# Splitting row maxima into bfloat16 parts by two truncating subtractions instead of four instructions, in a two-layer attention and feed-forward kernel

## The reference

```python
x = x + _L0_xattn_ref(_layernorm(x), ctx_2048, ...)   # attention in a band of 64, 8 heads of 8
x = x + _L0_ffn_ref(_layernorm(x), weight, scale)     # 256x256 product, row norm, tanh gain
x = x + _L1_xattn_ref(_layernorm(x), ctx_2048, ...)   # cross attention with rotary positions
x = x + _L1_ffn_ref(_layernorm(x), ...)               # 256 -> 1024 -> 256, relu, low-rank parts
```

## Time and profile before

| | |
|---|---|
| time, median of 3 runs | 1358.02 us (1356.0 to 1359.34) |
| the profiled execution | 1357.87 us, span of its instructions 1356.1 us |
| TensorE busy | 1272.2 us, 94% of the span |
| VectorE, ScalarE, GpSimd busy | 930.4, 854.8 and 709.6 us |
| attention of layer 0, steady part | about 100 to 500 us; an iteration takes some 15.5 us |
| attention of layer 1, steady part | about 620 to 1100 us; an iteration takes 15.5 us at first and 15.1 us later |
| last feed-forward | about 1140 us to the end |

### The profile page before, as it was taken

How to read it: one execution, slowest core, us unless ns; L and a number is a source line. 1 busy time by engine, 2 the same in 40 slices (tenths; PEclk the granted TensorE clock), 3 DMA queues, 4 the chain that set the end, 5 groups by cost and what they waited for, 6 DMA issues and landing times.

```text
span 1356.1 us, 36204 instructions
## 1 busy us (share of the span) xinstructions
PE 1272.2 (94%) x11164; PEld 833.3 (61%) x11164; DVE 930.4 (69%) x2052; ACT 854.8 (63%) x1849; POOL 709.6 (52%) x1297
## 2 busy tenths in 40 slices
PE   6999999999999997768999999999999989999998
PEld 3666666666666665544555556666666546666665
DVE  6888888888888874649899978888888852111110
ACT  2566666666667675556788878888888772222111
POOL 4577778777777865046555645556555410100000
PEclk9999999999999998987999989999999999999999
DMA  8554454444445440024344444444444400000000
GB/s 207 119 131 110 107 114 114 105 109 113 111 109 117 91 96 7 12 63 92 86 104 106 94 88 98 100 104 108 95 100 104 102 3 1 31 16 15 15 15 31
DMA packets 90487, 113.35 MB, mean 84 GB/s; under 512 B 13971, under 2 KB 80275, under 8 KB 82739
## 3 DMA queue, kind: packets, MB, share of 16 engines
q1 hardware_dynamic: 89216, 111.25, 35.2%
q10 hardware_dynamic: 1206, 1.29, 0.3%
HBM read 18.66 MB, written 4.19 MB: 17 GB/s over the span
## 4 chain that ended last, share of the span: by engine, by line
PE 75%; DVE 10%; issue 4%; POOL 4%; DMA 3%; ACT 3%; SPq 1%; POOLq 0%; DVEq 0%; ACTq 0%
PE bank L475 14%; PE bank L435 13%; PE bank L451 12%; PE bank L696 8%; PE bank L687 8%; PE bank L433 6%; PE bank L487 3%; DVE row_max L1136 3%; PE bank L506 2%; PE bank L538 2%; PE bank L527 2%; PE bank L516 2%; DMA Ks<-Ks 1%; PE bank L549 1%; PE bank L645 1%
## 5 line engine op out<-in xcount | busy, mean ns | idle before, releaser
L1136 DVE TENSOR_REDUCE row_max<-bank 128x2 f32<-128x384 f32 (+1 forms) x1024 | 594.4, 616 | 106.8 <-PE bank L435 102.9
L732 ACT ACTIVATE probs<-bank 128x384 f32<-128x384 f32 (+1 forms) x1024 | 539.5, 542 | 173.4 <-PE bank L451 160.3
L435 PE MATMUL bank<-Ks,Qs 96*128 96x192 bf16 (+1 forms) x2048 | 372.9, 264 | 11.3 <-DMA Ks<-Ks 6.2
L451 PE MATMUL bank<-Qs,Ks 128*128 128x192 bf16 (+1 forms) x2048 | 366.4, 260 | 13.7 <-ACT probs L732 12.4
L1360 POOL TENSOR_SCALAR_AFFINE_SELECT probs<-probs 128x256 f32<-128x256 f32 (+1 forms) x512 | 259.2, 530 | 112.4 <-ACT probs L732 91.9
L435 PEld LDWEIGHTS bank<-Ks,Qs 96*128 96x128 bf16 x2048 | 185.6, 99 | 126.8 <-DVE row_max L1136 43.1
L475 PE MATMUL bank<-probs,V 128*32 128x192 f32 (+1 forms) x4096 | 248.4, 360 | 5.4 <-POOL probs L1360 3.8
L451 PEld LDWEIGHTS bank<-Qs,Ks 128*128 128x128 bf16 x2048 | 185.7, 98 | 48.2 <-ACT probs L732 34.5
L433 PE MATMUL bank<-band,ident 128*128 128x384 bf16 x512 | 168.7, 330 | 2.5 <-DMA Ks<-Ks 2.0
L475 PEld LDWEIGHTS bank<-probs,V 128*32 128x32 f32 x4096 | 107.4, 109 | 84.4 <-issue 37.8
L1297 DVE TENSOR_TENSOR X<-bank,X 128x256 f32 (+1 forms) x32 | 13.6, 424 | 185.6 <-PE bank L696 185.6
(11 more groups left out here) (118 smaller groups left out, 1670.6 us busy)
## 6 DMA issues: line engine op xcount, KB each, us to landing
Ks<-Ks SPq DMA_DIRECT2D x64, 576.0 KB
Qs<-Qs SPq DMA_DIRECT2D x128, 192.0 KB
Qs<-Qp SPq DMA_DIRECT2D x192, 64.0 KB
Ks<-Kp SPq DMA_DIRECT2D x192, 64.0 KB
X<-in_x SPq DMA_DIRECT2D x4, 1024.0 KB, 13.4
side<-in_ctx_crossed SPq DMA_DIRECT2D x32, 128.0 KB, 2.1
side<-in_ctx SPq DMA_DIRECT2D x32, 128.0 KB, 2.1
out<-X SPq DMA_DIRECT2D x8, 512.0 KB, 3.0
```

What stands on the lines that cost most here:

```text
L435: last = nc.tensor.matmul(dst[:, blk * win:(blk + 1) * win], Qs[0:SHIFT_ROW, pair[1], h, blk * P:(blk + 1) * P], Ks[0:SHIFT_ROW, pair[1], ...
L451: last = nc.tensor.matmul(dst[:, blk * win:(blk + 1) * win], Ks[:, pair[1], h, blk * P:(blk + 1) * P], Qs[:, pair[1], h, start(blk):start( ...
L732: nc.scalar.activation(probs[:, h % 8, 0:2 * win], exp_bank[h % 2][:, 0:2 * win], ACT.Exp, scale=SCALE).then_inc(s["exped"], 1)
L1136: nc.vector.tensor_reduce(row_max[:, pair[1], h, :], bank_of(pair, h)[:, 0:2 * win].rearrange("p (b k) -> p b k", b=2), AX.X, ALU.max).the ...
```

## The change

The parts are now kept in float32 beside each other in `row_max`, which has a plane for each part, and the bfloat16 part is the *upper half* of each float32 number, read in place with a step of two (`upper`). The high part of a number is so its float32 form cut off at 16 bits, not rounded, and needs no instruction. The middle part is the upper half of `x - upper(x)`, and the last is the upper half of what the second subtraction leaves. Two of four instructions are left, `max_rest` and `max_last`. The wait for the turn of the pair before, which protected the old buffer, is gone, since `row_max` has room for three pairs.

```diff
-        row_max = sb("row_max", [P, RING, HPP, 2])
-        max_parts = sb("max_parts", [P, 2, PARTS, HPP], bf16)
-        max_rest = sb("max_rest", [P, 2, HPP])
+        row_max = sb("row_max", [P, RING, 2, PARTS, HPP])
...
+        def upper(part):
+
+            return part.bitcast(bf16)[:, 1::2]
...
-                for here in (slice(0, CH), slice(CH, P)):
+                for here in (slice(0, CH), slice(CH, P)) if l == 0 else (slice(0, P),):
                     last = nc.tensor.matmul(job_bank["B"][here, 0:T], w[here, WO, here], mixed_in[here, :],
                                             start=True, stop=True)
...
-                nc.tensor.transpose(max_bank[b], max_parts[:, half, :, :].rearrange("p n h -> p (n h)"),
+                nc.tensor.transpose(max_bank[b],
+                                    upper(row_max[:, pair[1], half, :, :].rearrange("p n h -> p (n h)")),
                                     ident16[:, :]).then_inc(s[f"{b}_filled"], 1)
...
-        def split_max(e, engine, s, l, pair, half):
+        def max_rest(e, engine, s, pair, half):
...
+            parts = row_max[:, pair[1], half, :, :]
+            wait_apart(e, (s["maxed"], num(pair) * HPP + HEADS * (half + 1)))
+            engine.tensor_tensor(parts[:, 1, :], parts[:, 0, :], upper(parts[:, 0, :]),
+                                 ALU.subtract).then_inc(s[f"max_step{half}"], 1)
+
+        def max_last(e, engine, s, pair, half):
...
+            parts = row_max[:, pair[1], half, :, :]
+            wait_apart(e, (s[f"max_step{half}"], num(pair) + 1))
+            engine.tensor_tensor(parts[:, 2, :], parts[:, 1, :], upper(parts[:, 1, :]),
                                  ALU.subtract).then_inc(s[f"max_parts{half}"], 1)
...
                     if l == 0 and h in (0, HEADS):
-                        split_max(e, nc.vector, s, l, p1 if h else r, 1 - h // HEADS)
+                        max_rest(e, nc.vector, s, p1 if h else r, 1 - h // HEADS)
+                    if l == 0 and h in (1, HEADS + 1):
+                        max_last(e, nc.vector, s, p1 if h > 1 else r, 1 - h // HEADS)
...
                     split("q", p3, Qp, q_rest, "q_mid", "q_parts")
-                    split_max(e, nc.gpsimd, s, l, p1, 0)
+                    max_rest(e, nc.gpsimd, s, p1, 0)
+                    max_last(e, nc.gpsimd, s, p1, 0)
                     split("k", p3, Kp, k_rest, "k_mid", "k_parts")
-                    split_max(e, nc.gpsimd, s, l, p1, 1)
+                    max_rest(e, nc.gpsimd, s, p1, 1)
+                    max_last(e, nc.gpsimd, s, p1, 1)
```

More of the change, by code:

```diff
@@ L985, in _ @@
                 relu_chunk(i * 2 + 1, 1)
-        def split_max(e, engine, s, l, pair, half):
+        def max_rest(e, engine, s, pair, half):
             if not active(pair):
                 return
[L991 to L1003, removed]
+            parts = row_max[:, pair[1], half, :, :]
[3 more added lines that the diff above has]
+        def max_last(e, engine, s, pair, half):
+            if not active(pair):
+                return
+            parts = row_max[:, pair[1], half, :, :]
+            wait_apart(e, (s[f"max_step{half}"], num(pair) + 1))
+            engine.tensor_tensor(parts[:, 2, :], parts[:, 1, :], upper(parts[:, 1, :]),
                                  ALU.subtract).then_inc(s[f"max_parts{half}"], 1)
@@ L1135, in maximum @@
                 e.wait_ge(s["scored"], num(pair) * HPP + h + 1)
-                nc.vector.tensor_reduce(row_max[:, pair[1], h, :],
+                nc.vector.tensor_reduce(row_max[:, pair[1], h // HEADS, 0, h % HEADS * 2:h % HEADS * 2 + 2],
                                         bank_of(pair, h)[:, 0:2 * win].rearrange("p (b k) -> p b k", b=2),
```

## The result

The changed kernel takes 1341.26 us (median of its runs) against 1358.43 us for the one before, measured beside it: a ratio of 0.9871, 95% interval 0.9849 to 0.9892. The profiled execution took 1342.02 us.

The account below looks back on a forecast made before the run. TensorE was taken as the bound in both attentions. Gains of 6.2 (layer 0's turn), 7.2 (projection) and 2.2 us (layer 1's split) sum to 15.6; from 1357.87 that gives 1342.3, rounded up to 1343 us, range 1337 to 1354.

Parts of the forecast that it names:

- The turn of half 1 in layer 0: TensorE's wait for the split on VectorE, shortened by 0.21 us a pair: 6.2 us over some 30 pairs.
- The turn of half 0: In layer 0, the turn at step 12 was said to have no wait to save: nothing gained.
- four steps of scores later: In layer 0, half 0's split at step 8 precedes its turn at step 12, so a shorter split saves nothing.
- VectorE's freed time: nothing: In layer 0, two copies fewer per split free VectorE, at 83.5% not the bound: no gain.
- The output projection: In layer 1, the step across it falls from 0.90 to 0.66 us: 0.24 a pair, 7.2 us for 30 pairs.
- the shorter split: On GpSimd in layer 1, parts 0.44 us earlier stay in time for step 12's turn, which TensorE reaches 0.24 earlier.
- rival 1: In layer 1 another engine, VectorE or ScalarE, takes the gain; only layer 0's 6.2 us remain: 1351.7 us, chance 0.14.
- The earlier turn in layer 1: Half 0's turn waits less for GpSimd's split: 0.24 us in 9 early pairs, 2.2 us; later iterations nothing.
- straight on: In layer 1's later iterations ScalarE goes from its copy directly to the exponentials, so an earlier turn gains nothing.
- the 9.4 us that were forecast for it: Layer 1's gain: 7.2 us from the output projection and 2.2 from the shorter split on GpSimd.
- The second: Rival: in layer 0 GpSimd's selects hold both subtractions in every phase, 4.8 us lost there: 1353.3 us, chance 0.12.
- The third: Rival: the turn's weight load with a step of two is slow, 0.12 us a turn cancelling the gain; chance 0.05.

Follow-up runs that it names:

- The fifth run: The kernel before the change, with layer 0's update of X at step 10 instead of step 11: 1355.22 us, ratio 0.9975 to the kernel before.
- the second run: The changed kernel with layer 1's output projection back in two products of 64 rows and columns: 1343.69 us, ratio 0.9893 to the kernel before.
- the first run: The kernel before with only layer 1's output projection made one product on 128 rows and columns: 1357.52 us, ratio 0.9995.
- the sixth run: The changed kernel with the second feed-forward update in layer 1's early iterations at step 15 instead of 11: 1336.42 us, ratio 0.9841 to the kernel before.
- the third run: The changed kernel with layer 0's second subtraction directly behind the first, no maximum between: 1333.12 us, ratio 0.9816 to the kernel before.

## Why the prediction was right, and where it was not

The time was forecast as 1343 us and is 1341.3 (1340.5 without the slowest execution). The sum was 15.6 us and the span lost 15.9. The chain of layer 0's turn and the shorter step across the projection came about as forecast; the other terms did not, and that the sum is so close is in part luck. Its terms:

- **The turn of half 1 in layer 0** was given 0.21 us a pair, 6.2 in all. The new chain is what was said: held `max_rest`, a maximum that TensorE's scores set, an unheld `max_last` in the gap before the fourth select. But it is 1.75 us in all phases, where I had 1.83 to 1.92. I had added up durations, and two VectorE instructions of which the second does not wait overlap by 0.09 us (the maximum starts at 319.32, `max_last` at 319.79, not 319.88). The turn's wait fell by 0.6, 0.24 and 0.13 us, 0.32 a pair.
- **The turn of half 0** was given nothing, "four steps of scores later". That step failed: the turn had a gap of 0.11 us a pair on average, which the view of waits doesn't show, since no view here lists a gap below 0.15 us. The fifth run showed that the turn's other wait, for the bank that the update reads, stood behind it. With it "VectorE's freed time: nothing" was wrong too.
- **Against both** stands GpSimd: every third iteration TensorE now waits 0.23 us for its masks. Together it is 0.37 us an iteration instead of 0.21. Layer 0's first iterations gave some of it back: the turns of half 1 of the fourth and the ninth pair are 0.8 and 0.9 us later than before, with a wait of 1.03 us for a DMA into `Ks` at 105.15 between them, which the second run, with the same layer 0, didn't have. The stage as a whole gained 7.3 us where 6.2 was forecast.
- **The output projection** was given 0.24 us a pair, and the step across it is 0.25 shorter. Both its parts went, as the rule of the Trainium skill on a change of tiling mode would have it (TensorEngine Tiling (Array Packing), "Key Properties"). But by the first run the projection alone is worth nothing. The prediction named the shorter split as what keeps the parts in time, and that is the very condition. It counted 30 pairs; in the 9 early ones the gain was lost to VectorE, rival 1 at work in a third of the layer.
- **The earlier turn in layer 1** was given 0.24 us in 9 early iterations and nothing in the later ones, and it went the other way round: 0.06 early, 0.13 later (the second run). Early, VectorE's feed-forward update at step 11 made the scores of step 14 wait 0.49 us, which the sixth run removed. Later, the claim that ScalarE goes "straight on" from its copy to the exponential rested on two rows that touch, 813.84 and 813.85. They touch by coincidence: in the iterations from 828 to 894 us ScalarE is idle for 0.09 us between the two, and the exponential starts 0.42 us after its shifted scores in the kernel before and after alike, so TensorE set it.
- That layer 1 gained the 9.4 us that were forecast for it is luck. The projection made about 4.8 instead of 7.2 (19 iterations at 0.25) and the earlier turn 3.0 instead of 2.2 (0.5 early, 2.5 later). The rest, about 1.6, has no term in the prediction: in the three iterations of the table the changed kernel gained 2.1 us, where a steady iteration gains at most 0.38, and the granted clock was below 1.00 in both traces and lower before in two of the three.

Of the rivals, the first was true for the early iterations only. The second, that selects hold both subtractions, did not happen with the maximum between them; in the third run it did, in every phase, and the kernel was faster all the same. The third is excluded by the load's 99 ns.

By the third run the maximum between the subtractions, which the change puts there, costs time. It fills a hand-over of 0.15 us with an instruction of 0.56 on the chain that TensorE waits for. And the 0.15 us themselves are the program's: in the loop `wait_apart` puts a semaphore increment between the wait and the instruction. Outside the loop, where it adds none, the second subtraction of the third run starts 0.03 us after the first. No run here tries the loop without the increment.

## What to carry to other kernels

An engine at 99% busy need not be the bound: shortening its work is worth nothing where it then waits for parts that come at a fixed time, and an edit that is worth nothing alone (the projection, 0.9995) can be worth its full 0.25 us an iteration once another has shortened what TensorE waits for. Ask of each gain on the busy engine which wait stands next behind it, and by how much it is met. Work placed between two dependent instructions to fill a hand-over belongs there only when the chain is not what others wait for. A gap of the busy engine that is too short for the view of waits may still be a wait, and at 0.1 us an iteration it adds up. Before a difference of some us between two runs is put down to an edit, compare the granted clock of the iterations in which it lies.

## What the runs showed of the hardware

- VectorE instructions with two SBUF inputs were held to the end of the GpSimd select that was running, up to 0.57 us for 0.17 us of work, and in the third run two in a row were. So was the first copy of the old split, with one SBUF input (0.57 us in the earlier trace rows). Maxima, which read PSUM, took 0.54 to 0.56 us whatever GpSimd did. That is the exclusive lock of the Trainium skill (SBUF — State Buffer, "SBUF: two separate sides"). The page has the port held for the whole instruction; beside GpSimd's TENSOR_SCALAR of 0.84 us (L1331 in the kernel before) the measurement differs. All 29 instructions of the split that started in its first 0.2 us ended 0.42 us after its start, but the last subtraction (L1003), where it started 0.45 us after it, took 0.17 to 0.18 us in all 24 cases, as if alone.
- A VectorE instruction that need not wait for the one ahead starts 0.09 us before that one's record ends. With a wait for it that stands directly at the instruction, it starts 0.03 us after, in all 64 splits of the kernel before (L999 behind L997); with a semaphore increment of the program between the wait and the instruction 0.15 us after (L1001 behind L999 in the loop). On GpSimd the same two are 0.08 and 0.20 us.
- A turn's weight load of 48 bfloat16 columns took 99 ns, contiguous or with a step of two.
- Going from a product on 128 rows and columns to one on 64 took 0.09 us more than to one of the same size.
